# Fourteen of 48 row pairs of h kept in SBUF instead of six, and the projection written out with kept and loaded pairs in turn

## The chip, the cores and the metric

The kernel is one program on one core of a Trainium2 chip. The time is the device time of one execution in microseconds (us); three runs of the kernel before are the reference for it. Engines are called as in the profile: PE multiplies matrices (PEld is its loading of weights), DVE and ACT work on vectors, POOL is the fourth engine, and SP issues most of the DMA transfers. SBUF is the memory on the core, PSUM the one into which PE writes, HBM the memory outside.

## What is computed

The input x has 8 images, 48 channels, 96 rows and 96 columns. Two layers follow each other. The first runs a convolutional LSTM down the rows and a second one up the rows, projects the two states h of every row to 48 channels, normalises over the batch, applies relu and adds x:

```python
hs_f = _convlstm_scan(xr, w_f[:, :, 1, :], b_f, reverse=False)
hs_b = _convlstm_scan(xr, w_b[:, :, 1, :], b_b, reverse=True)
feats = jnp.concatenate([hs_f, hs_b], axis=2)
y = jnp.einsum('oc,bchw->bohw', w_proj, feats)
mu = jnp.mean(y, axis=(0, 2, 3)); var = jnp.var(y, axis=(0, 2, 3))
y = gamma * (y - mu) * rsqrt(var + EPS) + beta
x1 = relu(y) + x
```

The second layer is a masked bottleneck on x1: a 1x1 convolution from 48 to 288 hidden channels of which 144 are chosen for each image, a 3x3 depthwise convolution, a 1x1 convolution back to 48, a mask, and x1 added.

```python
h = relu(bn1(conv1x1(x1, w_pw1))) * mask_dilate * vector[:, :, None, None]
h = relu(bnd(dwconv3x3(h, w_dw))) * mask
```

## The kernel before

The kernel is five stages with a barrier between each two: recurrence, projection, residual, gather, bottleneck.

**Recurrence.** 96 steps, each one row of the forward scan (partitions 0 to 63) and one row of the backward scan (partitions 64 to 127). A step's h is stored by SP (`store_h`, line 221). Rows are stored by pairs, 48 of them; one pair is 2 rows x 8 images x 96 columns of 128 partitions, 768 KB. A pair is complete only when both scans have passed it, so the first pairs are finished last. Pairs 0 to 2 and 45 to 47 go into SBUF (`h_kept`, 6 places at the start of the tensor `shared`, line 228); pairs 3 to 44 go to HBM (`h_rows`, line 230).

**Projection** (lines 491 to 582). Per row PE runs two matmuls, one for each half of the images, into one of eight PSUM banks (line 555; in the trace each such fp32 matmul shows as two MATMUL records, so a pair of rows is 8 records). ACT copies the bank into y (line 567), and DVE takes statistics of the row (line 578). The six kept pairs come first; then the 42 loaded ones, through four buffers `h_in` that SP fills (line 536). A load waits until PE is done with the pair that was in its buffer (`row_summed`), a pair's first matmul waits for its load (`h_loaded`). Two turns of four pairs and one more are written out, the other turns run in a loop. y is one tensor, [128, 4, 96 rows, 96].

**Residual** reads all of y twice and x_parts from HBM into `shared`. **Gather** prepares weights. **Bottleneck** (from line 1066) works in 12 chunks of 8 rows. PE runs, in an order written out by hand in lines 1294 to 1328, `pw1` (line 1211, 64 partitions of y by 128 columns of weights, one matmul for each half of the partitions), `pw1_b` (line 1221, four matmuls of 128 partitions by 32 columns), the taps of the depthwise convolution (line 1247) and `pw2` (lines 1269 to 1288). `pw1` and `pw1_b` read y directly: a chunk's ten rows as two jobs r = 0 and r = 1 of five rows each, that is 480 columns (`span`, line 1118), starting one row before the chunk's first.

Of the kernel before, what the change touches and what calls it, by code (L numbers as in the profile page):

```python
# [40 lines left out]
P = 128  # L41
# [18 lines left out]
KEPT = 3  # L60
KEPT_PX = 2 * B * W
CONSTS = 3 * P + HG + 2 * UNITS * UC
# [18 lines left out]
SHARED = max(2 * KEPT * KEPT_PX, WCOLS + 5 * H1_PX + CPX)  # L81


def carved(shared, at, *shape):

    size = 1
    for n in shape:
        size *= n
    flat = shared[:, at:at + size]
    if len(shape) == 1:  # L90
        return flat
    if len(shape) == 2:
        return flat.rearrange("p (a b) -> p a b", a=shape[0])
    return flat.rearrange("p (n a b c) -> p n a b c", n=shape[0], a=shape[1], b=shape[2])

# [7 lines left out]
def recurrence(nc, x_steps, w_gates, w_kinds, h_rows, x_lanes, x_parts, x_copied, h_kept, w_proj, wp, wp_loaded):  # L103
# [13 lines left out]
    with ExitStack() as ctx:  # L117
# [80 lines left out]
        def _(sp):  # L198
# [22 lines left out]
            def store_h(i, e):  # L221
                for d in range(2):
# [4 lines left out]
                    if isinstance(two, int) and not KEPT <= two < H // 2 - KEPT:  # L227
                        to = h_kept[own, two if two < KEPT else two - H // 2 + 2 * KEPT, row]
                    else:
                        to = h_rows[two, own, row]  # L230
# [260 lines left out]
def projection(nc, h_rows, h_kept, wp, wp_loaded, y, stats):  # L491

    ROWS, BUFS = 2, 4
    TURN = ROWS * BUFS
    TURNS = H // TURN
    HERE = 2 * KEPT
    SHORT = -(-HERE // BUFS)
    with ExitStack() as ctx:
# [4 lines left out]
        ps = ctx.enter_context(nc.psum_tensor("proj", [P, TURN, 512], F32))  # L503
# [4 lines left out]
        def pair_at(i, n):  # L508

            if isinstance(i, int) and BUFS * i + n < HERE:  # L510
                place = BUFS * i + n
                return place if place < KEPT else place - HERE + H // 2
            return i * BUFS + (n - KEPT)

        def row_at(i, k):
            return pair_at(i, k // ROWS) * ROWS + k % ROWS

        def loads_before(i, n):

            return i - sum(1 for j in range(SHORT) if BUFS * j + n < HERE)  # L520

        def turns(eng, body):
            for i in range(SHORT + 1):
                body(i)
            with eng.Fori(SHORT + 1, TURNS) as i:
                body(i)

        @block.sync
        def _(sp):
            def body(i):  # L530
                for n in range(BUFS):
                    if isinstance(i, int) and BUFS * i + n < HERE:
                        continue
                    if not isinstance(i, int) or loads_before(i, n):
                        sp.wait_ge(row_summed, TURN * (i - 1) + ROWS * (n + 1))
                    sp.dma_start(h_in[n][:], h_rows[pair_at(i, n)]).then_inc(h_loaded[n], 16)

            turns(sp, body)

        @block.tensor  # L540
        def _(pe):
            pe.wait_ge(wp_loaded, 16)

            def body(i):
                for k in range(TURN):
                    n = k // ROWS
                    if isinstance(i, int) and BUFS * i + n < HERE:
                        h = h_kept[:, BUFS * i + n]
                    else:
                        h = h_in[n]  # L550
                        if k % ROWS == 0:
                            pe.wait_ge(h_loaded[n], 16 * (loads_before(i, n) + 1))
                    at_least(pe, row_kept, TURN * (i - 1) + k + 1)
                    for half in range(2):
                        mm = nc.tensor.matmul(ps[64 * half:64 * half + 64, k, 0:NH], wp[:],
                                              h[:, k % ROWS, HB * half:HB * half + HB, :],
                                              start=True, stop=True)
                    mm.then_inc(row_summed, 1)

            turns(pe, body)  # L560

        @block.scalar
        def _(act):
            def body(i):
                for k in range(TURN):
                    act.wait_ge(row_summed, TURN * i + k + 1)
                    nc.scalar.activation(y[:, :, bass.ds(row_at(i, k), 1), :],
                                         ps[:, k, 0:NH].rearrange("p (b r w) -> p b r w", b=HB, r=1),
                                         ACT.Identity).then_inc(row_kept, 1)

            turns(act, body)

        @block.vector
        def _(dve):
            def body(i):
                for k in range(TURN):
                    dve.wait_ge(row_kept, TURN * i + k + 1)
                    nc.vector.bn_stats(stats[:, bass.ds(row_at(i, k) * 6, 6)],
                                       y[:, :, bass.ds(row_at(i, k), 1), :]).then_inc(row_measured, 1)

            turns(dve, body)
            dve.wait_ge(row_measured, H)

def residual(nc, shared, y, stats, consts, norms, x_parts, x_copied, sums, folded, prefetch, w_mask, b_mask, mask_rows, masks_stored,
# [10 lines left out]
    with ExitStack() as ctx:  # L597
# [52 lines left out]
        def own(i):  # L650
            return y[:, i % HB].rearrange("p r w -> p (r w)")[:, i // HB * PART:(i // HB + 1) * PART]
# [142 lines left out]
        def _(pe):  # L794
# [5 lines left out]
            def block_of(j, pairs):  # L800
                for pair in pairs:
                    for half in range(2):
                        lanes = slice(64 * half, 64 * half + 64)
                        mm = nc.tensor.matmul(logits[32 * pair:32 * pair + 32, half, :], w_one[lanes, 31 - j:63 - j],
                                              y[lanes, pair].rearrange("p r w -> p (r w)")[:, BLOCK * j:BLOCK * (j + 1)],
# [260 lines left out]
def bottleneck(nc, shared, y, out_lanes, packs, passes, mask_rows, masks_stored):  # L1066
# [8 lines left out]
    with ExitStack() as ctx:  # L1075
# [93 lines left out]
        def _(sp):  # L1169
# [4 lines left out]
            def masks(o):  # L1174
                for n in range(ALL_Z):
# [7 lines left out]
                    if o == 0:  # L1183

                        if c:
# [3 lines left out]
                                     y[0:HI + C, GROUPS[g]].rearrange("p r w -> p (r w)")[:, at:at + CPX]  # L1189
# [12 lines left out]
        def _(pe):  # L1202
            def one_pass(o):
# [495 lines left out]
```

## Time and profile before

| | |
|---|---|
| Time, median of 3 runs | 1727.27 us (1725.79 to 1729.94) |
| Span of the profiled execution | 1727.3 us |
| PE busy | 1616.2 us (94%) |
| ACT busy | 1264.7 us (73%) |
| DVE busy | 1192.9 us (69%) |
| Issues of h_in<-h_rows | 42 of 768 KB, 6.3 us to landing (median) |
| Issues of h_rows<-h_new | 168 of 192 KB, 2.7 us to landing (median) |

The profiled execution's own time is its span, 1727.3 us, which is the median of the runs to within 0.1 us, so nothing has to be added to a sum made against it. By the timeline, the recurrence ends with the barrier before 993.9 us, the projection runs from there to the barrier before 1090.9 us, the residual and gather stages to about 1188.9 us, and the bottleneck to the end. In the tables of windows DMA share is the mean busy share of the 16 DMA engines (sampling can put it a little over 1), and PEclk is the clock that PE was granted, 1.00 being 2.4 GHz and 0.50 being 1.2 GHz. A MATMUL record's own duration contains its fill and drain; the spacing of starts tells how fast PE goes through them.

### The profile page before, as it was taken

What the parts mean: (1) busy time and instruction counts of PE and PEld (TensorE: products, weight loads), DVE (VectorE), ACT (ScalarE), POOL (GpSimd) and SP (SyncE); (2) the same over time, 40 slices, a digit from 0 to 9 for tenths busy, and PEclk for the clock granted to TensorE, in tenths of its full rate; (3) what the DMA queues carried; (4) which work ended last, traced back from release to release, by engine and by line L of the source; (5) the groups of instructions that cost most, each with busy time, mean ns of one, the idle gap of its engine ahead of it and who ended that gap; (6) DMA issues with size and microseconds to landing.
All of it is one profiled execution on the core that took longest, in us unless ns stands there. A gap on an engine that the chain in (4) does not pass through costs nothing. (4 is left out here: it accounts for less than half of the span.)

```text
span 1727.3 us, 57365 instructions
## 1 busy us (share of the span) xinstructions
PE 1616.2 (94%) x23474; PEld 1246.9 (72%) x23474; DVE 1192.9 (69%) x1989; ACT 1264.7 (73%) x2393; POOL 110.9 (6%) x189
## 2 busy tenths in 40 slices
PE   6999999999999999999999877467999999999996
PEld 6999999999999999999999832124444444444443
DVE  5777777777777777777777655775666666666664
ACT  5888888888888888888888844754665566565563
POOL 4000000000000000000000000000000000000000
PEclk9999999999999999999999989776999999999998
DMA  5666566566666666666666489840233333333334
GB/s 149 167 170 165 156 170 167 165 161 170 176 168 165 165 169 163 170 167 163 162 172 168 120 314 389 342 185 14 61 81 80 80 81 80 81 80 81 78 82 89
DMA packets 97151, 257.69 MB, mean 149 GB/s; under 512 B 23048, under 2 KB 29084, under 8 KB 96924
## 3 DMA queue, kind: packets, MB, share of 16 engines
q1 hardware_dynamic: 85496, 219.86, 43.7%
q0 software_dynamic: 10880, 35.40, 10.1%
q8 instruction: 106, 1.74, 0.4%
q10 hardware_dynamic: 644, 0.49, 0.1%
q14 instruction: 25, 0.20, 0.0%
HBM read 127.03 MB, written 85.08 MB: 123 GB/s over the span
## 5 line engine op out<-in xcount | busy, mean ns | idle before, releaser
L288 PE MATMUL gates<-state,w_high 64*128 64x384 f32 x4608 | 504.4, 337 | 0.0
L288 PEld LDWEIGHTS gates<-state,w_high 64*128 64x128 f32 x4608 | 416.5, 185 | 0.0
L1247 PE MATMUL psd<-shared 32*32 32x384 f32 x10368 | 296.8, 491 | 2.1 <-issue 1.0
L288 PE MATMUL gates<-state,w_low 64*128 64x384 f32 x2304 | 267.6, 337 | 0.0
L1247 PEld LDWEIGHTS psd<-shared 32*32 32x32 f32 x10368 | 161.9, 103 | 135.6 <-issue 81.6
L288 PE MATMUL gates<-x_both,w_high 64*128 64x384 f32 x2304 | 237.3, 338 | 13.7 <-ACT w_high L342 13.7
L347 ACT ACTIVATE sig_f<-gates 48x384 f32<-48x384 f32 x384 | 187.0, 487 | 48.0 <-PE gates L288 42.8
L288 PEld LDWEIGHTS gates<-x_both,w_high 64*128 64x128 f32 x2304 | 207.5, 186 | 13.7 <-ACT w_high L342 13.7
L288 PEld LDWEIGHTS gates<-state,w_low 64*128 64x128 f32 x2304 | 208.6, 185 | 0.0
L1485 DVE SCALAR_TENSOR_TENSOR acc<-shared,acc 128x768 f32<-128x768 f32 x144 | 146.5, 1018 | 81.7 <-ACT acc L1395 77.9
L1485 DVE SCALAR_TENSOR_TENSOR acc<-h,shared,acc 128x768 f32<-128x768 f32 x144 | 146.5, 1017 | 73.7 <-ACT acc L1395 69.8
L347 ACT ACTIVATE sig_o<-gates 48x384 f32<-48x384 f32 x384 | 187.2, 487 | 7.0
L443 DVE TENSOR_TENSOR h_new<-sig_o,tanh_c 128x384 f32<-128x384 f32 x192 | 107.2, 558 | 122.3 <-ACT tanh_c L365 122.3
L347 ACT ACTIVATE sig_i<-gates 48x384 f32<-48x384 f32 x384 | 185.9, 484 | 7.0
L347 ACT ACTIVATE tanh_g<-gates 48x384 f32<-48x384 f32 x384 | 185.7, 484 | 7.0
L1367 ACT ACTIVATE shared<-ps,shared 128x480 f32<-128x480 f32 (+1 forms) x176 | 123.4, 744 | 71.7 <-PE ps L1217 52.2
L432 DVE TENSOR_TENSOR i_g<-sig_i,tanh_g 128x384 f32<-128x384 f32 x192 | 107.2, 558 | 93.6 <-ACT tanh_g L347 93.6
L365 ACT ACTIVATE tanh_c<-cell 128x384 f32<-128x384 f32 x192 | 100.8, 525 | 53.1 <-DVE cell L435 53.1
L435 DVE TENSOR_TENSOR cell<-f_c,i_g 128x384 f32<-128x384 f32 x192 | 107.2, 558 | 20.0
L396 DVE TENSOR_TENSOR state<-h_new,state 128x384 fp32r<-128x384 f32 x192 | 107.2, 558 | 6.7
L428 DVE TENSOR_TENSOR f_c<-sig_f,cell 128x384 f32<-128x384 f32 x192 | 105.9, 551 | 5.4 <-ACT sig_f L347 5.4
L1217 PE MATMUL ps<-y,shared 64*128 64x480 f32 (+1 forms) x380 | 102.9, 612 | 5.4 <-SPq L1170 3.5
(153 smaller groups left out, 1620.8 us busy)
## 6 DMA issues: line engine op xcount, KB each, us to landing
x_taps<-x_both SPq DMA_DIRECT2D x192, 195.5 KB, 3.3
x_raw<-x_steps SPq DMA_DIRECT2D x192, 192.0 KB, 3.2
h_rows<-h_new SPq DMA_DIRECT2D x168, 192.0 KB, 2.7
h_in<-h_rows SPq DMA_DIRECT2D x42, 768.0 KB, 6.3
x_last<-x_both SPq DMA_DIRECT2D x192, 98.0 KB, 3.0
shared<-x_parts SPq DMA_DIRECT2D x24, 768.0 KB, 9.3
out<-y SPq DMA_DIRECT2D x48, 336.0 KB, 5.5
out<-z POOLq DMA_DIRECT2D x47, 336.0 KB, 5.6
```

Of the source, the lines that this page charges most:

```text
L288: return nc.tensor.matmul(gates[p][d][:, m, 0:NH], w[own, n, m, :], moving[own], start=start, stop=stop)
L347: return nc.scalar.activation(out[at], gates[p][d][col:col + HC, m, 0:NH].rearrange("p (b w) -> p b w", b=HB), func)
L365: nc.scalar.activation(tanh_c[p][:], cell[p][:], ACT.Tanh).then_inc(tc_ready, 1)
L396: nc.vector.tensor_tensor(state[1 - e][:, 1, b, 1:1 + W], h_new[e][:, b], state[1 - e][:, 0, b, 1:1 + W].bitcast(F32), ALU.subtract).then_ ...
L428: nc.vector.tensor_tensor(f_c[p][:], sig_f[p][:], cell[p][:], ALU.mult).then_inc(fc_ready, 1)
L432: nc.vector.tensor_tensor(i_g[p][:], sig_i[p][:], tanh_g[p][:], ALU.mult).then_inc(ig_ready, 1)
L435: nc.vector.tensor_tensor(cell[p][:], f_c[p][:], i_g[p][:], ALU.add).then_inc(cell_ready, 1)
L443: nc.vector.tensor_tensor(h_new[e][:, halves(p)], sig_o[e][:, halves(p)], tanh_c[p][:], ALU.mult).then_inc(h_ready, 1)
L1217: mm = nc.tensor.matmul(bank_of(j, half)[:, 0:(hi - lo) * W], wt[own, W_A + P * pair:W_A + P * (pair + 1)], y[own, pair, lo:hi, :], start= ...
L1247: mm = nc.tensor.matmul(psd[lane:lane + 32, 2 * x + i, 0:NH], wt[own, to:to + 32], h1p[2 * (s % 2) + x][own, dy + 4 * m:dy + 4 * m + 4, dx ...
L1367: return nc.scalar.activation(h1[:, first:first + hi - lo, 1:1 + W], bank[:, 0:(hi - lo) * W].rearrange("p (r w) -> p r w", w=W), ACT.Relu ...
L1485: nc.vector.scalar_tensor_tensor(a, window(h1d[d % 2], tap), par(D_UNITS[s], TAP + tap), a, ALU.mult, ALU.add).then_inc(acc_done if tap == ...
```

## The change

`KEPT` goes from 3 to 7, so pairs 0 to 6 and 41 to 47 stay in SBUF and 34 pairs are written to HBM and loaded. y becomes two tensors: `y_head` with rows 0 to 63 and `y_tail` with rows 64 to 95. y_tail is allocated before the recurrence, and the first eight kept places lie in it (`IN_TAIL` = 8); the other six lie in `shared`, whose size is unchanged. The projection is written out fully for PE, ACT, DVE and SP, in the order of a list: two kept pairs, then twelve times two loaded pairs and a kept one, then ten loaded pairs. Where the bottleneck reads rows on both sides of row 64, one matmul becomes two.

```diff
-KEPT = 3
+KEPT = 7
 KEPT_PX = 2 * B * W
+HEAD = 64
+IN_TAIL = (H - HEAD) * HB * W // KEPT_PX
...
-SHARED = max(2 * KEPT * KEPT_PX, WCOLS + 5 * H1_PX + CPX)
+SHARED = max((2 * KEPT - IN_TAIL) * KEPT_PX, WCOLS + 5 * H1_PX + CPX)
...
+def y_rows(y, lanes, pair, lo, hi):
+    head, tail = y
+    runs = []
+    if lo < HEAD:
+        runs.append((0, head[lanes, pair, lo:min(hi, HEAD), :]))
+    if hi > HEAD:
+        first = max(lo, HEAD)
+        runs.append(((first - lo) * W, tail[lanes, pair, first - HEAD:hi - HEAD, :]))
+    return [(at, ap, ap.shape[1] * W) for at, ap in runs]
...
+    ORDER = [("kept", 0), ("kept", 1)]
+    for n, pair in enumerate(LOADED):
+        ORDER.append(("loaded", pair))
+        if n % 2 == 1 and 2 + n // 2 < HERE:
+            ORDER.append(("kept", 2 + n // 2))
...
+            for pair in LOADED:
+                n = USE[pair]
+                if n >= BUFS:
+                    sp.wait_ge(row_summed, ROWS * (AT[pair - BUFS] + 1))
+                sp.dma_start(h_in[n % BUFS][:], h_rows[pair]).then_inc(h_loaded[n % BUFS], 16)
...
+            for k in range(H):
+                kind, n = ORDER[k // ROWS]
+                if kind == "kept":
+                    h = h_kept(n)
+                else:
+                    h = h_in[USE[n] % BUFS]
+                    if k % ROWS == 0:
+                        pe.wait_ge(h_loaded[USE[n] % BUFS], 16 * (USE[n] // BUFS + 1))
+                at_least(pe, row_kept, k - BANKS + 1)
+                for half in range(2):
+                    mm = nc.tensor.matmul(ps[64 * half:64 * half + 64, k % BANKS, 0:NH], wp[:],
+                                          h[:, k % ROWS, HB * half:HB * half + HB, :],
+                                          start=True, stop=True)
+                mm.then_inc(row_summed, 1)
...
-                        mm = nc.tensor.matmul(bank_of(j, half)[:, 0:(hi - lo) * W], wt[own, W_A + P * pair:W_A + P * (pair + 1)],
-                                              y[own, pair, lo:hi, :], start=True, stop=True)
+                        for at, x1, count in y_rows(y, own, pair, lo, hi):
+                            mm = nc.tensor.matmul(bank_of(j, half)[:, at:at + count], wt[own, W_A + P * pair:W_A + P * (pair + 1)],
+                                                  x1, start=True, stop=True)
...
+            if place < IN_TAIL:
+                flat = y_tail[:].rearrange("p b r w -> p (b r w)")[:, place * KEPT_PX:(place + 1) * KEPT_PX]
+            else:
+                flat = shared[:, (place - IN_TAIL) * KEPT_PX:(place - IN_TAIL + 1) * KEPT_PX]
```

`pw1_b` changes in the same way as `pw1`; the logits of the residual stage and the stores of y read blocks that row 64 never divides. Of the ten loaded pairs at the end, the first is pair 31.

PE at the start of the projection, before (`proj` are the PSUM banks, `shared` holds the kept pairs, `h_in` the loaded ones; a row of the list is one or more matmuls of the program):

```order
160 L555 MATMUL proj<-shared,wp 64x384 [waits wp_loaded]
161 L555 MATMUL proj<-shared,wp 64x384 x15
162 L555 MATMUL proj<-shared,wp 64x384 [waits row_kept]
163 L555 MATMUL proj<-shared,wp 64x384
164 L555 MATMUL proj<-shared,wp 64x384 [waits row_kept]
165 L555 MATMUL proj<-shared,wp 64x384
166 L555 MATMUL proj<-shared,wp 64x384 [waits row_kept]
167 L555 MATMUL proj<-shared,wp 64x384
168 L555 MATMUL proj<-shared,wp 64x384 [waits row_kept]
169 L555 MATMUL proj<-shared,wp 64x384
170 L555 MATMUL proj<-h_in,wp 64x384 [waits row_kept,h_loaded2]
171 L555 MATMUL proj<-h_in,wp 64x384
```

and now (`y_tail` holds kept pairs here):

```order
160 L579 MATMUL proj<-y_tail,wp 64x384 [waits wp_loaded]
161 L579 MATMUL proj<-y_tail,wp 64x384 x7
162 L579 MATMUL proj<-h_in,wp 64x384 [waits h_loaded0]
163 L579 MATMUL proj<-h_in,wp 64x384 x3
164 L579 MATMUL proj<-h_in,wp 64x384 [waits h_loaded1]
165 L579 MATMUL proj<-h_in,wp 64x384 x3
166 L579 MATMUL proj<-y_tail,wp 64x384 [waits row_kept]
167 L579 MATMUL proj<-y_tail,wp 64x384
168 L579 MATMUL proj<-y_tail,wp 64x384 [waits row_kept]
169 L579 MATMUL proj<-y_tail,wp 64x384
170 L579 MATMUL proj<-h_in,wp 64x384 [waits row_kept,h_loaded2]
171 L579 MATMUL proj<-h_in,wp 64x384
```

Six kept pairs, 24 matmuls, stood ahead of the first loaded pair; now two kept pairs, 8 matmuls, do, and from there each third pair is a kept one.

SP at the same place, before (`h_rows` is in HBM):

```order
149 L536 DMA h_in<-h_rows 128x1536 x4
150 L536 DMA h_in<-h_rows 128x1536 [waits row_summed] x2
151 L525 UNCONDITIONAL_BRANCH
152 L525 ISA
153 L536 ISA [waits row_summed]
154 L536 DMA h_in<-h_rows 128x1536
155 L535 REGISTER_ALU
156 L536 ISA [waits row_summed]
157 L536 DMA h_in<-h_rows 128x1536
158 L535 REGISTER_ALU
159 L536 ISA [waits row_summed]
```

and now:

```order
259 L148 UNCONDITIONAL_BRANCH [waits h_stored1,h_stored0]
260 L557 UNCONDITIONAL_BRANCH [waits barrier_Pool_Activation_PE_DVE_SP_release]
261 L564 DMA h_in<-h_rows 128x1536 x4
262 L564 DMA h_in<-h_rows 128x1536 [waits row_summed] x30
263 L538 UNCONDITIONAL_BRANCH
```

Four loads still go out without a wait, and the rest with a wait each. Of these there were 38; now there are 30.

PE in the bottleneck where job r = 1 of a chunk ends at row 64, before (`ps` and `psd` are PSUM, `shared` holds weights and the depthwise input):

```order
579 L1247 MATMUL psd<-shared 32x384 [waits relu2p_done,relu1_done]
580 L1247 MATMUL psd<-shared 32x384 x47
581 L1217 MATMUL ps<-y,shared 128x480 [waits relu1_done] x2
582 L1247 MATMUL psd<-shared 32x384 x96
583 L1217 MATMUL ps<-y,shared 128x480 [waits relu1_done] x2
```

and the same place now:

```order
757 L1262 MATMUL psd<-shared 32x384 x47
758 L1231 MATMUL ps<-y_head,shared 128x384 [waits relu1_done]
759 L1231 MATMUL ps<-y_tail,shared 128x96
760 L1231 MATMUL ps<-y_head,shared 128x384 [waits relu1_done]
761 L1231 MATMUL ps<-y_tail,shared 128x96
762 L1262 MATMUL psd<-shared 32x384 x96
763 L1231 MATMUL ps<-y_head,shared 128x96 [waits relu1_done]
764 L1231 MATMUL ps<-y_tail,shared 128x384
765 L1231 MATMUL ps<-y_head,shared 128x96 [waits relu1_done]
766 L1231 MATMUL ps<-y_tail,shared 128x384
```

The matmul of 480 columns of each half has become one of 384 and one of 96, with the same weights; both pieces of one half stand ahead of the first piece of the other half. The next job's are 96 and then 384.

## Rows read from the trace of the kernel before

**Rows 1.** Windows: stretch, its us, busy us, PEclk, DMA share, GB/s

```profile
core 0: us, PE busy (x) PEld busy (x) DVE busy (x) ACT busy (x) POOL busy (x), PEclk, DMA share, GB/s
1010.00:1015.00 5.00, 3.76 (x14) 1.51 (x16) 0.93 (x2) 1.02 (x3) 0.00 (x0) 0.66 0.92 385
...
1050.00:1060.00 10.00, 7.50 (x42) 2.50 (x40) 5.37 (x10) 4.90 (x10) 0.00 (x0) 1.00 1.00 400
...
1495.00:1538.00 43.00, 43.00 (x988) 19.53 (x984) 27.81 (x28) 25.95 (x39) 3.27 (x4) 1.00 0.39 81
```

**Rows 2.** Waits, 994 to 1091: total us, times, longest

```profile
PE proj L555 <- DMA h_in<-h_rows: 17.6, 28, 2.5
```

**Rows 3.** Timeline of PE, projection: start, us, instructions, idle before

```profile
993.95 9.59 PE L555 MATMUL proj<-shared,wp 128*64 128x384 f32 x48 [7.82 <-PEq L117]
1003.36 5.34 PE L555 MATMUL proj<-h_in,wp 128*64 128x384 f32 x32
1011.24 7.24 PE L555 MATMUL proj<-h_in,wp 128*64 128x384 f32 x32 [2.54 <-DMA h_in<-h_rows]
...
1029.48 1.51 PE L555 MATMUL proj<-h_in,wp 128*64 128x384 f32 x8 [1.60 <-DMA h_in<-h_rows]
1031.88 1.51 PE L555 MATMUL proj<-h_in,wp 128*64 128x384 f32 x8 [0.89 <-DMA h_in<-h_rows]
...
1087.47 1.51 PE L555 MATMUL proj<-h_in,wp 128*64 128x384 f32 x8 [0.45 <-DMA h_in<-h_rows]
```

**Rows 4.** Timeline, all engines, start of projection

```profile
995.53 0.49 ACT L567 ACTIVATE y<-proj 128x384 f32<-128x384 f32 x1 [6.17 <-PE proj L555]
...
998.42 0.49 ACT L567 ACTIVATE y<-proj 128x384 f32<-128x384 f32 x1 [0.15 <-PE proj L555]
...
1008.74 0.49 ACT L567 ACTIVATE y<-proj 128x384 f32<-128x384 f32 x1 [0.15 <-PE proj L555]
```

**Rows 5.** Timeline, SP's second batch of loads

```profile
1004.86 4.37 SPq L536 DMA_DIRECT2D h_in<-h_rows  x4
```

**Rows 6.** Landing of h_in loads issued 993.9, 995.2, and 1040 to 1060

```profile
DMA to landing us min/median/max: 4.4/4.4/4.4
...
DMA to landing us min/median/max: 7.3/8.0/8.7
...
DMA to landing us min/median/max: 5.8/6.1/6.5
```

**Rows 7.** Timeline of PE, bottleneck: two widths of line 1217, and 1226

```profile
1202.52 0.92 PE L1217 MATMUL ps<-y,shared 64*128 64x384 f32 x4
...
1206.07 1.07 PE L1217 MATMUL ps<-y,shared 64*128 64x480 f32 x4
...
1227.65 1.82 PE L1226 MATMUL ps<-y,shared 128*32 128x480 f32 x16
```

**Rows 8.** Chain of waits, 1560 to 1580: start, us, what

```profile
1567.53 1.00 PE ps L1217 x4
...
1572.92 1.75 PE ps L1226 x16
```

**Rows 9.** Waits of PE, 1200 to the end, longest of five

```profile
PE psd L1247 <- issue: 1.0, 3, 0.6
```

**Rows 10.** Timeline of PE, small matmuls of line 959

```profile
1183.95 1.51 PE L959 MATMUL ps_tail<-par,onehot_b 96*32 96x64 f32 x48
```

**Rows 11.** Timeline of PEld, weights for one pair of line 1217

```profile
1206.07 0.30 PEld L1217 LDWEIGHTS ps<-y,shared 64*128 64x128 f32 x4 [0.62 <-ACT shared L1367]
```

**Rows 12.** DMA issues 25 to 900: count, KB, us to landing

```profile
h_rows<-h_new SPq DMA_DIRECT2D x160, 192.0 KB, 2.7
...
shared<-h_new SPq DMA_DIRECT2D x12, 192.0 KB, 3.3
```

**Rows 13.** DMA queue of instructions, 1300 to 1400: packets, MB

```profile
q8 instruction: 18, 0.29, 1.2%
```

**Rows 14.** Windows, 1300 to 1400, columns as in rows 1

```profile
1300.00:1400.00 100.00, 99.78 (x2337) 45.80 (x2316) 68.58 (x70) 59.42 (x88) 8.18 (x10) 1.00 0.38 80
```

More of the change, by code:

```diff
@@ L94, in carved, with y_flat, kept_pair, kept_place @@
     return flat.rearrange("p (n a b c) -> p n a b c", n=shape[0], a=shape[1], b=shape[2])
+def y_rows(y, lanes, pair, lo, hi):
[7 more added lines that the diff above has]
+    return [(at, ap, ap.shape[1] * W) for at, ap in runs]
+def y_flat(y, lanes, pair, at, count):
+    head, tail = y
+    part, base = (head, 0) if at < HEAD * W else (tail, HEAD * W)
+    return part[lanes, pair].rearrange("p r w -> p (r w)")[:, at - base:at - base + count]
+def kept_pair(place):
+    return place if place < KEPT else place - 2 * KEPT + H // 2
+def kept_place(pair):
+    return pair if pair < KEPT else pair - H // 2 + 2 * KEPT
 def at_least(eng, sem, value):
@@ L227, in store_h @@
                     if isinstance(two, int) and not KEPT <= two < H // 2 - KEPT:
-                        to = h_kept[own, two if two < KEPT else two - H // 2 + 2 * KEPT, row]
+                        to = h_kept(kept_place(two))[own, row]
                     else:
@@ L491, in projection @@
 def projection(nc, h_rows, h_kept, wp, wp_loaded, y, stats):
-    ROWS, BUFS = 2, 4
-    TURN = ROWS * BUFS
-    TURNS = H // TURN
+    ROWS, BUFS, BANKS = 2, 4, 8
     HERE = 2 * KEPT
-    SHORT = -(-HERE // BUFS)
+    LOADED = range(KEPT, H // 2 - KEPT)
+    ORDER = [("kept", 0), ("kept", 1)]
[3 more added lines that the diff above has]
+            ORDER.append(("kept", 2 + n // 2))
+    assert sum(1 for kind, _ in ORDER if kind == "kept") == HERE and len(ORDER) == H // 2
+    USE = {pair: n for n, pair in enumerate(LOADED)}
+    AT = {pair: n for n, (kind, pair) in enumerate(ORDER) if kind == "loaded"}
     with ExitStack() as ctx:
@@ L506, in projection, with row_of, y_row @@
         block = ctx.enter_context(nc.Block())
[L508 to L526, printed above, removed]
+        def row_of(k):
+            kind, n = ORDER[k // ROWS]
+            return (n if kind == "loaded" else kept_pair(n)) * ROWS + k % ROWS
+        def y_row(row):
+            head, tail = y
+            return head[:, :, row, :] if row < HEAD else tail[:, :, row - HEAD, :]
         @block.sync
         def _(sp):
[L530 to L538, printed above, removed]
+            for pair in LOADED:
[3 more added lines that the diff above has]
+                sp.dma_start(h_in[n % BUFS][:], h_rows[pair]).then_inc(h_loaded[n % BUFS], 16)
         @block.tensor
@@ L542, in _ @@
             pe.wait_ge(wp_loaded, 16)
[L544 to L558, printed above, removed]
@@ L562, in _ @@
         @block.scalar
         def _(act):
[L564 to L571, printed above, removed]
+            for k in range(H):
+                act.wait_ge(row_summed, k + 1)
+                nc.scalar.activation(y_row(row_of(k)), ps[:, k % BANKS, 0:NH].rearrange("p (b w) -> p b w", b=HB),
+                                     ACT.Identity).then_inc(row_kept, 1)
@@ L573, in _ @@
         @block.vector
         def _(dve):
[L575 to L581, printed above, removed]
+            for k in range(H):
+                dve.wait_ge(row_kept, k + 1)
+                nc.vector.bn_stats(stats[:, 6 * row_of(k):6 * row_of(k) + 6], y_row(row_of(k))).then_inc(row_measured, 1)
@@ L1225, in pw1_b @@
                         for pair in range(HB):
[L1226 to L1228 removed]
+                            for at, x1, count in y_rows(y, slice(0, P), pair, lo, hi):
+                                mm = nc.tensor.matmul(bank_of(job_b(c), r)[32 * pair:32 * pair + 32, at:at + count],
+                                                      wt[:, W_B + 32 * pair:W_B + 32 * (pair + 1)],
+                                                      x1, start=True, stop=True)
                     mm.then_inc(pw1_done, 1)
```

20 lines of the change are left out of this document (10 added, 10 removed).

## The prediction

> **What bounds the kernel now.** I read the slices of the page first, then a table of windows, then waits and timeline of the two places that the change touches. In the windows the reader is to see two different kernels. In the projection, from 1050 to 1060, the DMA engines are busy all of the time at 400 GB/s and PE only 7.50 us of 10; in the bottleneck, from 1495 to 1538, PE is busy 43.00 of 43 us and the DMA share is 0.39 [rows 1]. So in the projection bytes count, in the bottleneck PE's instructions. The waits agree: in the projection PE waits 17.6 us in 28 pieces for h_in [rows 2], while from 1200 on the longest total of its waits is 1.0 us [rows 9].
>
> The timeline of PE gives the rhythm of the projection [rows 3]. Six kept pairs and the first four loaded ones run from 993.95 to 1008.7 without a wait. Then come two bursts of four pairs, starting at 1011.24 and, after 18.24 us for eight pairs, at 1029.48: 2.28 us a pair. From 1031.88 to the last pair at 1087.47 the 29 pairs start one by one, 28 steps of 1.985 us, each held by its load. That is the steady rate of the loads. The bursts are a result of the order: the first four loads all went out at once, the second four only at 1004.86 and after, since PE was busy with kept pairs [rows 5]; the last of the first four landed by 995.2 + 8.7 = 1003.9 [rows 6], so for a while no load was under way, and later four buffers ran in step. In a burst the clock is low as well: 0.66 from 1010 to 1015, a mix of 1.2 and 2.4 GHz [rows 1].
>
> PE's own rate: ACT copies each row as PE finishes it, at 998.42 and again at 1008.74, 16 rows later, so 0.645 us a row or 1.29 us a pair at 2.4 GHz [rows 4]. The first copy stands at 995.53, 1.6 us after PE's start, at the low clock.
>
> **The projection, step by step.** Removed are 8 of 42 loads. What ends the stage is then the later of two chains.
> - The loads. The first one lands at 993.9 + 4.4 = 998.3 [rows 6]; two kept pairs cover it, since their four rows are done about then [rows 4]. With 1.985 us for each of the other 33 the last pair can start at 998.3 + 33 x 1.985 = 1063.8. Before it started at 1087.47 [rows 3]. Gain 23.7 us.
> - PE. From row 4 on there are 92 rows of 0.645 us = 59.3 us after 998.4; its last pair would start at 998.4 + 59.3 - 1.3 = 1056.4, which is 31.1 us earlier than before. It is the end of the range on the fast side, if the loads ran so fast.
>
> Why the loads should stay at their steady rate: the interleaving asks of them two pairs in the time in which PE does three, 3.87 us, and they need 2 x 1.985 = 3.97 us. So both are busy nearly all of the time. From PE's release of a buffer until PE wants it again lie three loaded pairs and two kept ones, 5 x 1.29 = 6.45 us, and a load of the steady phase lands after 5.8 to 6.5 us [rows 6]. It fits with nothing to spare, so I let the loads decide. In the ten loaded pairs at the end nothing lies between; that is the steady phase of before. The bad end is the rate of the bursts throughout: 998.3 + 33 x 2.28 = 1073.5, gain 14.0 us. I take 1.985, for it comes from 28 steps under the same queue.
>
> The Trainium skill, in DMA: Bandwidth & Descriptors (the table at its head), gives about 358 GB/s as one core's limit from HBM. The trace disagrees: 400 GB/s over 10 us [rows 1], and the measurement decides. By the page's figure a pair of 786,432 bytes would take 2.20 us, an estimate, the last pair would start at 1070.9, and the gain would be 16.6 us.
>
> The tail behind the last pair (copy, statistics, barrier) is the same code and moves with it. Writing the loop out takes register instructions off ACT and DVE, which wait for PE anyway: nothing.
>
> **Stores in the recurrence.** Eight more pairs, 32 stores of 192 KB, go to SBUF. Such a store lands after 3.3 us against 2.7 us to HBM [rows 12], and is next waited for a pair of steps later, some 20 us. Same count, same queue, same place: nothing, with 1 us to either side. The last store before the barrier went to SBUF before too.
>
> **The bottleneck: what the split of y costs.** Rows 60 to 64 (chunk 7, r = 1) and 63 to 67 (chunk 8, r = 0) lie across row 64. That makes 2 x 4 pairs of `pw1`, two halves each, and 2 x 4 matmuls of `pw1_b`: 24 matmuls become 48. PE has no waits there to hide them, so each us is lost. No row shows two matmuls of one part of the array in a row ahead of the other part's, so I bound.
> - Widths: a `pw1` job of 384 columns has 0.92 us in the timeline, one of 480 columns 1.07 us [rows 7], so 96 columns are about 0.16 us; the job takes 1.00 us of the chain [rows 8], that is 0.80 of columns with both halves side by side and 0.20 fixed.
> - If the second half can't start until the first half's second piece does: 384 then 96 takes 0.64 + 0.64 + 0.16 + 0.20 = 1.64 instead of 1.00, so 0.64 more; 96 then 384 takes 0.16 + 0.16 + 0.64 + 0.20 = 1.16, 0.16 more. Four of each: 3.2 us. `pw1_b` takes 1.75 us for both r [rows 8], four matmuls side by side in 0.80 of columns. In turn, they become 4 x 0.64 + 0.16 = 2.72 (1.92 more) and 4 x 0.16 + 0.64 = 1.28 (0.48 more): 2.4 us. Together 5.6 us.
> - Low end: the pieces run as freely as the 24 small matmuls of line 959, 1.51 us for 24 [rows 10]: 1.5 us. High end: the serial 5.6 us, and the weights of the 16 added `pw1` pieces, 0.30 us for two halves [rows 11], uncovered: 8 x 0.30 = 2.4, so 8.0 us.
>
> I take 5.6 us: PE is given its matmuls in program order, and the two pieces of one half need the same part of the array.
>
> On this the Trainium skill has two rules that point in two directions. TensorE: Matmul & The Clock Gate (Part 3, what overlaps) says that matmuls start and end in program order and that a weight load passes running matmuls only in another row group; by that the sum holds 5.6 us or more. TensorEngine Tiling (Key Properties) says that tiles work independently of each other; by that it would hold nearer 1.5 us. No run so far shows which.
>
> **Sum.** 1727.3 (span, equal to the median) - 23.7 + 5.6 = 1709.2 us.
>
> **Rivals.**
> - *Fast.* The pieces overlap (1.5 us) and the loads hold 1.985: 1727.3 - 23.7 + 1.5 = 1705.1. With PE as the bound of the projection instead, 1727.3 - 31.1 + 1.5 = 1697.7. For it speaks that the four records of a `pw1` job load all their weights within 0.30 us [rows 11]; against the second part, that the DMA engines were full already at 400 GB/s.
> - *Bursts stay.* If uneven release of buffers (two pairs 1.29 us apart, then a gap) keeps the loads at 2.28 us: 1727.3 - 14.0 + 5.6 = 1718.9. For it: 18 us of this in the trace. Against: it followed a gap with no load under way, and the new order has none.
> - *Slower: instruction blocks.* The written-out projection streams its instructions by DMA, behind the loads. In the bottleneck 18 packets came for 2337 + 2316 + 70 + 88 instructions [rows 13, 14], about 270 each; the projection has 768 of PE and 192 of ACT and DVE and so brings 4 packets or more. If each was late by a load's landing, 6.3 us, and they added up, that is 25 us and the time 1709.2 + 25 = 1734. It decides from three late packets on (18.1 us of net gain / 6.3). Against: the first 24 rows are written out already, and their PE rows run at 0.645 us without a gap [rows 4].
> - *No change to speak of.* A gain at the low end with a late packet or two: 1718.9 + 6.3 = 1725.
>
> **Chances.** Forecast 1709 as it stands: 0.52. Fast: 0.25. Bursts stay: 0.15. No change: 0.04. Slower: 0.04. Runs of this kernel lie within 0.2%, about 3.5 us, of each other, and within that is no change. Faster 0.92, same 0.04, slower 0.04. For 8 in 10 the range takes the forecast with the ends of the split (1705 to 1712), goes down into the fast case without all of PE's bound, and up to the bursts: 1701 to 1719.
>
> **What will show it.** The kernel is right step by step if the last loaded pair starts near 1063.8 and loads go at 1.9 to 2.0 us each; if no PE gap lies between 998 and the first turns, with PEclk 1.00 from there; if `pw1` with two pieces takes 1.6 us in chunk 7 and 1.2 in chunk 8, `pw1_b` 2.7 and 1.3; and if chunks 0 to 6 and 9 to 11 and the recurrence keep their lengths. The prediction is wrong if a load takes 2.2 us or more, if ACT or PE stand still in the projection with no semaphore to wait for, or if the recurrence is longer.

## The result and the profile after

The changed kernel takes 1709.1 us (median of 4 runs, 1708.4 to 1711.0) against 1726.6 us of the kernel before (median of 4); the ratio is 0.9894 with a 95% interval of 0.988 to 0.9908. Two later comparisons (e9_again and e10_after_3, below) gave 0.9902 (0.9873 to 0.9931) and 0.991 (0.9883 to 0.9936), so the medians differ by 14 to 17 us. The profiled execution has a span of 1706.6 us and took 1708.7 us.

PE's timeline in the projection, kernel after (start, us, what, idle time before and what ended it), answers to [rows 3]:

```profile
991.66 5.32 PE L579 MATMUL proj<-y_tail,wp 128*64 128x384 f32 x16 [7.83 <-PEq L148]
996.79 2.76 PE L579 MATMUL proj<-h_in,wp 128*64 128x384 f32 x16
999.38 1.47 PE L579 MATMUL proj<-y_tail,wp 128*64 128x384 f32 x8
...
1044.96 1.46 PE L579 MATMUL proj<-shared,wp 128*64 128x384 f32 x8
1046.25 2.75 PE L579 MATMUL proj<-h_in,wp 128*64 128x384 f32 x16
1050.04 1.51 PE L579 MATMUL proj<-h_in,wp 128*64 128x384 f32 x8 [1.04 <-DMA h_in<-h_rows]
1051.91 1.51 PE L579 MATMUL proj<-h_in,wp 128*64 128x384 f32 x8 [0.35 <-DMA h_in<-h_rows]
...
1063.68 1.51 PE L579 MATMUL proj<-h_in,wp 128*64 128x384 f32 x8 [0.37 <-DMA h_in<-h_rows]
```

The first load is there when two kept pairs are done, nothing waits at 996.79, and the last pair starts 72.0 us after PE's first matmul, where it was 93.5. The waits of PE between 991 and 1065, against [rows 2]:

```profile
PE proj L579 <- DMA h_in<-h_rows: 5.6, 12, 1.0
```

The 17.6 us in 28 pieces are 5.6 in 12. Windows of the interleaved part (columns as in [rows 1]):

```profile
1011.66:1031.66 20.00, 19.39 (x120) 8.07 (x118) 16.74 (x31) 14.70 (x30) 0.00 (x0) 1.00 0.96 372
1031.66:1051.66 20.00, 18.55 (x112) 7.40 (x108) 15.25 (x28) 13.29 (x28) 0.00 (x0) 1.00 0.98 386
```

PE is busy 93 to 97% there, where it was 75% [rows 1], and the DMA engines still are busy almost all of the time. In the bottleneck, the two jobs that lie across row 64, in the timeline of PE after:

```profile
1494.84 0.92 PE L1231 MATMUL ps<-y_head,shared 64*128 64x384 f32 x4
1495.59 0.37 PE L1231 MATMUL ps<-y_tail,shared 64*128 64x96 f32 x4
1495.89 5.30 PE L1262 MATMUL psd<-shared 32*32 32x384 f32 x192
1501.12 0.47 PE L1231 MATMUL ps<-y_head,shared 64*128 64x96 f32 x4
1501.41 0.85 PE L1231 MATMUL ps<-y_tail,shared 64*128 64x384 f32 x4
...
1509.88 0.39 PE L1241 MATMUL ps<-y_head,shared 128*32 128x96 f32 x8
1510.07 1.65 PE L1241 MATMUL ps<-y_tail,shared 128*32 128x384 f32 x16
1511.65 1.15 PE L1262 MATMUL psd<-shared 32*32 32x384 f32 x33
```

From a job's first record to the next instruction it takes 1.05 us (384 then 96 columns) and 1.07 us (1501.12 to 1502.19, 96 then 384), `pw1_b` 1.77 us; undivided they took 1.00 and 1.75 [rows 8]. The forecast was 1.64 and 1.16 for the two orders of pieces, and 1.75 + 0.48 = 2.23 for this `pw1_b`, of whose two jobs one is divided, 96 columns first.

By stages, the first pair of profiles, in us:

| | before | after | difference |
|---|---|---|---|
| Recurrence, up to PE's first projection matmul | 993.95 | 991.66 | -2.3 |
| Projection, from there to bn_aggr | 97.0 | 75.2 | -21.8 |
| Residual and gather, to the first pw1 | 98.0 | 98.1 | +0.1 |
| Bottleneck, to the end | 538.3 | 541.6 | +3.3 |

One execution is too little for this. Over all profiles of this study PE's first projection matmul came between 990.4 and 994.1 with either store pattern (991.6 and 994.1 in two kernels with the old recurrence, 993.4 and 992.9 in two more executions of the changed one), so the -2.3 is the execution's. For the projection three profiles with the old code (97.0, 95.1, 94.5) stand against three with the new (75.2, 76.3, 76.4): 95.5 against 76.0, a gain of 19.6 us. (A fourth profile with the old order and the old 42 loads, e5_unroll_only below, had 97.9; with it the gain is 20.2.)

### The profile page after: what moved, and what is told of

Same layout as the page of the kernel before. It is cut to its first block and busy times, and to the rows that moved or that the text cites. A ratio compares the mean times of both kernels' runs of the same rounds, so it can differ in the third digit from the quotient of the medians.

```text
span 1706.6 us, 56613 instructions
## 1 busy us (share of the span) xinstructions
PE 1613.0 (95%) x23522; PEld 1253.0 (73%) x23522; DVE 1193.5 (70%) x1989; ACT 1265.0 (74%) x2393; POOL 110.5 (6%) x189
## 5 line engine op out<-in xcount | busy, mean ns | idle before, releaser
L1500 DVE SCALAR_TENSOR_TENSOR acc<-h,shared,acc 128x768 f32<-128x768 f32 x144 | 146.5, 1018 | 73.3 <-ACT acc L1410 69.4
L1382 ACT ACTIVATE shared<-ps,shared 128x480 f32<-128x480 f32 (+1 forms) x176 | 123.3, 743 | 72.3 <-PE ps L1231 52.8
L319 PE MATMUL gates<-x_last,w_low 64*128 64x384 f32 x768 | 102.1, 344 | 1.0 <-DMA x_last<-x_both 0.6
```

What stands on the lines that cost most here:

```text
L319: return nc.tensor.matmul(gates[p][d][:, m, 0:NH], w[own, n, m, :], moving[own], start=start, stop=stop)
L1382: return nc.scalar.activation(h1[:, first:first + hi - lo, 1:1 + W], bank[:, 0:(hi - lo) * W].rearrange("p (r w) -> p r w", w=W), ACT.Relu ...
L1500: nc.vector.scalar_tensor_tensor(a, window(h1d[d % 2], tap), par(D_UNITS[s], TAP + tap), a, ALU.mult, ALU.add).then_inc(acc_done if tap == ...
```

## The experiments

Each was compared with the kernel before on its own chip. "Last pair" is the start of the last loaded pair after PE's first matmul of the projection, "projection" the time from that matmul to bn_aggr, "bottleneck" the time from the first `pw1` to the end; these three are of one profiled execution each. The kernel before took 1728.2 us beside e1, e2, e4 and e5, 1728.1 us beside e3, e6, e8 and e9, and 1727.4 us beside e10 and v1.

| | time, us | ratio to before, 95% | last pair | projection | bottleneck |
|---|---|---|---|---|---|
| e1_split_all | 1738.1 | 1.0054 (1.0039 to 1.0069) | 91.7 | 95.1 | 552.5 |
| e2_split_64 | 1730.9 | 1.0016 (1.0003 to 1.0029) | 91.0 | 94.5 | 540.9 |
| e5_unroll_only | 1729.0 | 1.0009 (0.9994 to 1.0023) | 94.7 | 97.9 | 540.1 |
| e4_order_only | 1724.1 | 0.9988 (0.9969 to 1.0008) | 86.5 | 89.6 | 543.9 |
| e3_kept_first | 1725.2 | 0.9979 (0.9962 to 0.9996) | 86.0 | 89.2 | 540.3 |
| e6_half_bytes | 1701.0 | 0.9835 (0.9806 to 0.9864) | 62.6 | 66.1 | 542.0 |
| e8_bufs3 | 1727.1 | 0.999 (0.9975 to 1.0005) | 87.9 | 91.0 | 544.4 |
| e9_again (the changed kernel) | 1712.3 | 0.9902 (0.9873 to 0.9931) | 73.2 | 76.3 | 543.4 |
| e10_after_3 (the changed kernel) | 1713.2 | 0.991 (0.9883 to 0.9936) | 73.3 | 76.4 | 543.9 |
| v1_keep18 | 1705.5 | 0.9864 (0.9838 to 0.989) | 66.3 | 69.5 | 545.4 |

### What the split of y costs

e1_split_all, on the kernel before:

```diff
-mm = nc.tensor.matmul(bank_of(j, half)[:, 0:(hi - lo) * W], wt[own, ...], y[own, pair, lo:hi, :], ...)
+mid = lo + 1 if r == 0 else hi - 1
+for a, b in [(lo, mid), (mid, hi)]:
+    mm = nc.tensor.matmul(bank_of(j, half)[:, (a - lo) * W:(b - lo) * W], wt[own, ...], y[own, pair, a:b, :], ...)
```

and the same in `pw1_b`. In e2_split_64 only the jobs across row 64 are cut, there.

> The kernel before, with nothing changed but this: in every chunk of the bottleneck each matmul of pw1 and of pw1_b is cut into two pieces, 96 columns and the rest (r = 0) or the rest and 96 (r = 1). All 12 chunks then pay what the changed kernel pays for two jobs' rows. Theory A (pieces of one part of the array hold up the other parts, as the prediction had it): about 0.16 us more per pw1 job at r = 0, 0.64 at r = 1 and 2.4 for both jobs of pw1_b, so 12 x (4 x 0.16 + 4 x 0.64 + 2.4) = about 67 us more than before, 1794 us. Theory B (each part of the array works through its own pieces, from the changed kernel's trace about 0.05 us per pw1 job and next to nothing for pw1_b): 96 x 0.05 = about 5 us more, 1732 us. In between, at some 0.2 us per job, it would be 20 us.

> The kernel before, with only the matmuls that lie across row 64 of y cut there (chunk 7 r = 1, chunk 8 r = 0), so the changed kernel's 24 added matmuls and nothing else of it. Theory A (serial pieces): 5.6 us more than before, 1733 us. Theory B (independent parts): 0.5 us more, not to be told from 0. The changed kernel's bottleneck was 3.3 us longer in its profile; if the split is the cause of that in some other way than by its own duration, it shows here as 3 us.

Cutting all twelve chunks costs 9.3 us (6.7 to 11.9), not 67: 0.78 us (0.56 to 0.99) for a chunk's 24 added matmuls, and 24 added matmuls are all that the change has. The timeline of PE in e1_split_all:

```profile
1401.71 1.87 PE L1233 MATMUL ps<-y,shared 128*32 128x96 f32 x32
1403.51 4.33 PE L1254 MATMUL psd<-shared 32*32 32x384 f32 x128
1407.77 1.15 PE L1222 MATMUL ps<-y,shared 64*128 64x96 f32 x8
1408.85 0.54 PE L1276 MATMUL ps<-h2p,shared 64*64 64x384 f32 x2
```

`pw1_b` takes 1.80 us to the next instruction, a `pw1` job 1.08: some 0.05 and 0.08 more than undivided [rows 8], and 8 x 0.08 + 0.05 = 0.7 a chunk. The serial theory is refuted. e2_split_64 came out 2.8 us slower (0.5 to 5.0), which excludes 5.6, and from 0.78 can't be told.

### Order, number of loads and the written-out code

```diff
 e5_unroll_only, on the kernel after
-KEPT = 7
+KEPT = 3
-IN_TAIL = (H - HEAD) * HB * W // KEPT_PX
+IN_TAIL = 0
-ORDER = [two kept, then two loaded and a kept one in turn]
+ORDER = [("kept", n) for n in range(HERE)] + [("loaded", pair) for pair in LOADED]
```

e4_order_only has the first two edits alone, e3_kept_first the last alone.

> The changed kernel with 6 kept pairs as before, none in y's tail, and the kept ones projected first: the order and the bytes of before, written out instead of looped, and y still split. Theory A (written-out code costs nothing, as its instructions come ahead of need): within 1 us of before, last pair 93.5 us after PE's first matmul of the projection. Theory B (instruction blocks come late behind the loads): one to four waits of some 6 us, 1733 us or more. Theory C (the loop itself cost something per pair, so part of the gain came from its end): faster than before by 1 to 4 us.

> The changed kernel with 6 kept pairs as before (42 loads, none in y's tail), but in the new interleaved order: two kept, then loaded ones with a kept one after every second until the kept ones are used up. Theory A (the loads run without a break from the first landing on, 1.985 us each): the last pair starts at 998.3 + 41 x 1.985 = 1079.7 on the scale of before, 7.8 us earlier than before, so about 1720 us. Theory B (only the number of loads counts and the order is worth nothing): as before, 1727. If the four-pair bursts at 2.28 us stay, 998.3 + 41 x 2.28 = 1091.8, so 1732.

> The changed kernel with all 14 kept pairs projected first and the 34 loaded ones after them; same bytes, same stores, same code otherwise. Theory A (the gain needs the interleaving, since the loads stand still once four buffers are full): PE starts the first loaded pair after 28 rows of 0.645 us = some 19 us, 4 loads are there, and 30 more have to follow at 1.985 us from then on, so the last pair starts some 13 us later than in the changed kernel, 1722 us; with bursts at 2.28 us for the first eight some 15 us. Theory B (eight loads fewer are worth 8 x 1.985 = 16 us whatever the order): 1711 us, and no more than 2 us over the changed kernel.

Written out, the old order takes the old time (between 1.0 us less and 4.0 more), so the loop cost nothing and no instruction block came late; "Slower" is refuted. The new order with the old 42 loads starts the last pair 8.2 us earlier than e5, as expected (7.8), though its time is only 4.9 us less; against the kernel before the time alone doesn't show a gain (ratio 0.9969 to 1.0008). Eight fewer loads in the old order bring 2.9 us (0.7 to 6.6 by the interval of the ratio) instead of 14 to 17; with all kept pairs first the kernel is 12.8 us slower than e9_again on the same chip, where theory A had 13. The timeline of PE in e3_kept_first shows why:

```profile
993.29 12.56 PE L575 MATMUL proj<-y_tail,wp 128*64 128x384 f32 x64 [7.83 <-PEq L148]
1005.68 7.92 PE L575 MATMUL proj<-shared,wp 128*64 128x384 f32 x48
1013.42 5.34 PE L575 MATMUL proj<-h_in,wp 128*64 128x384 f32 x32
```

and its windows of the same stretch (columns as in [rows 1]):

```profile
1003.29:1008.29 5.00, 5.00 (x34) 2.33 (x32) 4.38 (x8) 3.89 (x8) 0.00 (x0) 1.00 0.01 2
1008.29:1013.29 5.00, 5.00 (x34) 2.42 (x32) 4.35 (x8) 3.76 (x9) 0.00 (x0) 1.00 0.00 0
```

For ten microseconds nothing is loaded: all four buffers are full and PE is busy with kept pairs. The kept pairs are worth their loads where they lie between the loaded ones. With the old order most of what they save goes into a longer gap.

### What bounds the new projection

```diff
 e6_half_bytes, on the kernel after (leaves out half of the loaded bytes)
-sp.dma_start(h_in[n % BUFS][:], h_rows[pair])
+sp.dma_start(h_in[n % BUFS][:, 0:1], h_rows[pair, :, 0:1])
-h[:, k % ROWS, ...]
+h[:, 0 if kind == "loaded" else k % ROWS, ...]
 e8_bufs3, on the kernel after
-ROWS, BUFS, BANKS = 2, 4, 8
+ROWS, BUFS, BANKS = 2, 3, 8
```

> The changed kernel, but each load brings only the first row of its pair, and the second row's matmuls read the first row again: half of the loaded bytes and half of the loaded rows are left out, the matmuls and their order are the same. Theory A (the loads bound the projection): PE becomes the bound, 0.645 us a row, and the last pair starts at 1056.4 on the scale of before, 7.3 us earlier than in the changed kernel, so about 1702 us. Theory B (PE was the bound of most of it already and the loads cost only its last ten pairs): those ten go from 1.89 to 1.29 us each, 6 us, 1703 us; the two differ in where the time goes: by A before and in the last ten pairs, by B in the last ten alone. Theory C (latency or the rhythm of buffers bounds it, not bytes): less than 2 us gained.

> The changed kernel with three buffers for loaded pairs instead of four. Theory A (three loads under way are enough to keep the DMA engines full, bytes decide): within 2 us of the changed kernel. Theory B (a load's own time of 6.4 us from issue to landing decides: with three buffers a load can start only after the third pair before it was projected, so a pair of loads' time is (6.4 + 1.29) / 3 = 2.56 us where nothing lies between): the last ten pairs go from 1.89 to about 2.5 us, 6 us, and the interleaved part loses too; 10 to 20 us in all, 1719 to 1729 us.

With half of the bytes PE doesn't wait for a load at all, and the time is 11.3 us less than that of e9_again on the same chip, so theory C is refuted. PE's timeline ends:

```profile
1042.16 1.47 PE L579 MATMUL proj<-shared,wp 128*64 128x384 f32 x8
1043.45 13.42 PE L579 MATMUL proj<-h_in,wp 128*64 128x384 f32 x80
```

Ten pairs at 1.29 us, the last at 1043.45 + 9 x 1.29 = 1055.1, 62.6 us after PE's first matmul; the forecast floor was 1056.4 - 993.95 = 62.5. The changed kernel is 10 us above it: it reaches the ten last pairs after 54.6 us (1046.25) where e6 needs 51.0, and spends 17.4 us on nine steps where e6 spends 11.6. So theory A holds: the loads bound both parts, the last ten pairs more. What e6 doesn't separate is bytes and waiting time, since its loads also landed sooner, after 3.7 us instead of 6.4.

Three buffers cost 14.8 us against e9_again on the same chip. In the last pairs (timeline of PE in e8_bufs3)

```profile
1061.84 1.51 PE L579 MATMUL proj<-h_in,wp 128*64 128x384 f32 x8 [0.56 <-DMA h_in<-h_rows]
...
1079.38 1.51 PE L579 MATMUL proj<-h_in,wp 128*64 128x384 f32 x8 [0.42 <-DMA h_in<-h_rows]
```

seven steps take 17.54 us, 2.51 each (expected 2.56); singly they are 1.9 to 3.2 us. The DMA engines are not full there (windows):

```profile
1061.84:1079.38 17.54, 10.58 (x57) 3.40 (x57) 7.79 (x14) 6.75 (x14) 0.00 (x0) 1.00 0.82 306
```

and a load still takes 5.9 us to land (median of the 34), not much less than the 6.4 with four buffers. So with three buffers the time from issue to landing decides, as theory B had it; A is refuted. That with four it is the bytes rests on the DMA share of 0.96 to 0.98 in the changed kernel's windows; five buffers, which would have settled it, were not tried.

### Run to run

> The changed kernel again, for a second profile of it. The recurrence was 2.3 us shorter in its profile than in that of the kernel before, the bottleneck 3.3 us longer; if these are the run's own, they vary here by about that (recurrence up to PE's first projection matmul at 991.7 to 994), and the clock rows at the bottleneck's start with them. If they belong to the change they stand: 991.7 and 541.6 us.

> The changed kernel on the same chip as the version with 18 kept pairs, so that the two can be compared directly: 1709 to 1712 us, last pair 72 to 73.2 us after PE's start.

The recurrence varied as expected and the projection stood. The time of e10_after_3, 1713.2 us, lies a little above the expected 1709 to 1712. The bottleneck did not come back to 541.6: 543.4 and 543.9. Its parts show two places. In the first chunk, the windows of 20 us that begin 20 us after its first matmul, kernel after:

```profile
1184.97:1204.97 20.00, 19.12 (x441) 9.50 (x456) 15.88 (x16) 14.84 (x24) 0.88 (x1) 0.91 0.08 13
```

and e9_again:

```profile
1187.64:1207.64 20.00, 19.69 (x499) 9.66 (x498) 17.14 (x17) 13.52 (x22) 0.88 (x1) 1.00 0.18 36
```

A mean granted clock of 0.91, a mix of the two levels of 1.2 and 2.4 GHz, instead of 1.00 goes with a first chunk of 38.3 us instead of 35.6; the first profile of the changed kernel and e10_after_3 had it, the others not. And the last stretch, from the twelfth `pw1_b` to the end, took 67.0 and 66.9 us in the first two profiles and 67.7 to 72.3 in the others. The traces show what is longer there: DVE's idle time, most of it for transfers. The last three outputs in the timeline of DVE, kernel before:

```profile
1706.20 1.02 DVE L1495 SCALAR_TENSOR_TENSOR z<-ps,shared,mask 128x768 f32<-128x768 f32 x1 [1.17 <-DMA mask<-mask_rows]
1710.54 1.02 DVE L1495 SCALAR_TENSOR_TENSOR acc<-ps,shared,mask 128x768 f32<-128x768 f32 x1 [3.32 <-PE ps L1286]
1715.79 1.02 DVE L1495 SCALAR_TENSOR_TENSOR z<-ps,shared,mask 128x768 f32<-128x768 f32 x1 [4.23 <-DMA mask<-mask_rows]
```

and e9_again:

```profile
1686.59 1.02 DVE L1510 SCALAR_TENSOR_TENSOR z<-ps,shared,mask 128x768 f32<-128x768 f32 x1 [3.36 <-DMA out<-z]
1692.96 1.02 DVE L1510 SCALAR_TENSOR_TENSOR acc<-ps,shared,mask 128x768 f32<-128x768 f32 x1 [5.34 <-DMA mask<-mask_rows]
1698.19 1.02 DVE L1510 SCALAR_TENSOR_TENSOR z<-ps,shared,mask 128x768 f32<-128x768 f32 x1 [4.21 <-DMA mask<-mask_rows]
```

That is 8.7 us of idle time against 12.9, and from the last of these outputs to the end it is 11.5 us against 12.8. The changed kernel's first profile, the same program as e9_again, had 9.9 and 11.2, so this is scatter from one execution to the next and not the change. Why the transfers land later in some executions is open. The four stretches from the eighth `pw1_b` to the twelfth, in which nearly all of the split lies, took 173.9 us before and 173.9, 174.0 and 174.1 in the three profiles of the changed kernel: what is late around row 64 (up to 1.3 us) is made up in the next chunks. Of the executions with kept pairs first, four had bottlenecks of 538.3 to 540.9; the seven with pairs in turn had 541.6 to 545.4. The fifth with kept pairs first is e1_split_all: its 552.5 less the 8 to 9 us of its cut matmuls is 543 to 544, in the other group. So the order is a doubtful cause; I know of no mechanism for it and tested none.

### A further version

```diff
 v1_keep18, on the kernel after
-KEPT = 7
-HEAD = 64
+KEPT = 9
+HEAD = 48
+PLACES = [45, 0, 1, 46, 2, 3, 47, 4, 5, 6, 7, 8, 39, 40, 41, 42, 43, 44]
...
+    kept = [p for p in range(IN_TAIL) if PLACES[p] < KEPT] + [p for p in range(IN_TAIL) if PLACES[p] > KEPT]
+    kept += range(IN_TAIL, HERE)
+    ORDER = [("kept", kept.pop(0)), ("kept", kept.pop(0))]
+    for n, pair in enumerate(LOADED):
+        ORDER.append(("loaded", pair))
+        if kept and (n < 2 * KEPT and n % 3 != 2 or n >= 2 * KEPT and n % 2 == 1):
+            ORDER.append(("kept", kept.pop(0)))
```

> A further version: 18 kept pairs instead of 14, 30 loaded; y is cut at row 48 instead of 64, its rows 48 to 95 hold 12 of the kept pairs until they are projected, and the order takes a kept pair after every loaded one or two at first (all 12 are read before y's row 48 or higher is written over them), so that loads and PE have about the same work. Theory (bytes bound the changed kernel's projection, PE's own floor is 9 to 10 us below, as with half of the bytes): the loads need 4.4 + 29 x 1.985 = 62.0 us from PE's start to the last pair's start, PE's own rows 62.6 us; with both this close some 64 us, against 72.0 and 73.2 of the changed kernel, so 8 to 9 us less, 1701 to 1704 us. The stores of 8 more rows' pairs to SBUF cost nothing and the cut of y 0.5 us as before. Rival (no rate but the number of kept pairs in the interleaving counts, or writing next to y's kept pairs adds waits): 4 loads less are worth 4 x 1.985 = 8 us only if PE keeps up, else nothing: 1710.

It takes 1705.5 us (five runs, 1698.7 to 1707.9) where the changed kernel takes 1713.2 (four, 1707.8 to 1714.1) on the same chip: 7.7 us less, where 8 to 9 less and 1701 to 1704 us had been expected. The last pair starts after 66.3 us, 2.3 us later than expected. Waits of PE, 990 to 1060:

```profile
PE proj L584 <- DMA h_in<-h_rows: 2.1, 5, 0.7
```

Little is left to gain from loads: PE's own floor of 62.6 us is 3.7 us away.

## Why the prediction was right, and where it was wrong

**Time: 1709.2 forecast, 1709.1 measured.** The mechanism of the gain was right: loads and kept pairs in turn, the loads as the bound. That of the cost of the split was wrong. The two terms were off by 4 to 5 us each in opposite directions, and the agreement to 0.1 us is chance.

**The basis.** I took the span of 1727.3 us as the execution's own time. In every execution for which both are known the time is 1.9 to 2.2 us above the span (1708.67 and 1706.6 here), so the profiled execution of before took about 1729.3 us, and is not the run of the median; the nearest of the reference runs is the one of 1729.94. The sum should have had 2 us added for that, and 2 us taken off again to reach the median; the two cancel.

**The loads, -23.7.** The step said 4.35 us to the first landing and 33 x 1.985 = 65.5, so 69.9 us to the last pair. Measured are 72.0, 73.2 and 73.3. The first landing is right (no wait at 996.79). The rate is not quite (nor was it the 2.20 us worked out from the Trainium skill, DMA: Bandwidth & Descriptors, the table at its head): (72.8 - 4.4) / 33 = 2.07 us a load over three profiles. That is 3.0 us, and it is the term that was mis-sized. The 1.985 was one execution's rate. From the 13th loaded pair to the last, 29 steps with nothing between, the kernels with the old order and 42 loads took 58.0 us (before), 57.5 (e1), 56.6 (e2) and 60.6 (e5), so 1.95 to 2.09 us a load; e4_order_only, with four kept pairs among its first loads, needs (1078.30 - 996.19) / 41 = 2.00. In the changed kernel the last seven steps, also with nothing between, took 1.95, 2.13 and 1.96 us each in the three profiles. So 2.07 lies within the scatter of the loads themselves, and whether the uneven release of buffers between kept pairs adds to it is not shown, though "it fits with nothing to spare" left no room for either. A further 1.5 us was in the kernel before: its profiled execution had 93.5 us to the last pair, two others 91.0 and 91.7. 23.7 - 3.0 - 1.5 = 19.2, and the profiles' means give 92.1 - 72.8 = 19.3.

**The bursts.** I read them as the result of the gap in the loads, and the low clock as something beside it. For the time that holds, for the pattern it doesn't. The eight pairs that took 18.24 us in two bursts, from the fifth loaded pair to the 13th, took 17.87 us in e1, 18.05 in e2 and 18.43 in e5, all three with the same order, singly and at a granted clock of 1.00. So 2.28 us a pair is the price of getting going again after the gap, and the bursts add nothing to it. What makes four pairs run together is the clock: in e3_kept_first a burst stands in the middle of a steady stretch, with no gap in the loads, behind a wait of 1.94 us of PE (timeline, then windows):

```profile
1044.80 7.18 PE L575 MATMUL proj<-h_in,wp 128*64 128x384 f32 x32 [1.94 <-DMA h_in<-h_rows]
```

```profile
1042.80:1044.80 2.00, 0.07 (x2) 0.00 (x0) 1.11 (x2) 0.49 (x1) 0.00 (x0) 1.00 1.02 418
1044.80:1048.80 4.00, 4.00 (x14) 1.57 (x16) 1.12 (x2) 1.18 (x3) 0.00 (x0) 0.57 0.91 350
1048.80:1052.80 4.00, 3.61 (x24) 1.31 (x22) 3.05 (x6) 2.74 (x6) 0.00 (x0) 1.00 0.98 330
```

PE came back at a granted clock of 0.57, between its levels of 1.2 and 2.4 GHz, after nearly standing still, and took four pairs without a wait; the next one started at 1052.37, after 7.57 us, which is four steps of 1.89. The burst cost nothing; the long step ahead of it did. A burst doesn't always follow: in e2_split_64 a wait of 2.25 us was followed by a granted clock of 1.00, and so was one of 1.92 us in the changed kernel (timeline, then windows of e10_after_3):

```profile
1052.47 1.51 PE L579 MATMUL proj<-h_in,wp 128*64 128x384 f32 x8 [1.92 <-DMA h_in<-h_rows]
```

```profile
1052.47:1056.47 4.00, 3.27 (x18) 1.16 (x20) 1.73 (x4) 1.96 (x4) 0.00 (x0) 1.00 1.01 349
```

"Bursts stay" at 2.28 us a load did not happen: the new order has no gap in the loads.

**The split, +5.6.** This term failed, at the step "PE is given its matmuls in program order, and the two pieces of one half need the same part of the array". Each half goes on by itself. In program order the first half's short piece stands ahead of the second half's long one. In the trace of the first job above the long pieces of both halves start together, one line of 0.92 us as in a job of 384 columns [rows 7], and the short ones of both start behind them, at 1495.59. The whole job takes 1.05 us, not 1.64. The price is 0.5 us by the changed kernel's own rows (8 jobs of 0.05 to 0.07 and 0.02 for `pw1_b`) and 0.8 us by e1_split_all; the "low end" of 1.5 was still too high. Of the two rules of the Trainium skill quoted in the prediction, TensorEngine Tiling (Key Properties), by which tiles work independently, agrees with these runs; the in-order rule of TensorE: Matmul & The Clock Gate (Part 3) is not what they show: the second half's long piece started about 0.7 us before the first half's short one. I should have given the independent case more than the 0.25 of "Fast", all the more as `pw1_b` was seen to run four matmuls side by side.

**Recurrence, code, residual.** All priced at nothing; the runs show nothing beyond their scatter. The fetching of instructions, which carried the slower rival, brought 3 packets in the new projection against 1 and no wait (e5_unroll_only).

**The balance.** -19.3 and +0.8 make -18.5 us; the three comparisons gave -17.4, -15.8 and -14.2. The profiles put the remaining 1 to 4 us into the bottleneck's first chunk (2.6 us in two of three, with the lower clock) and its end (4.6 us in one of three, with DVE's longer waits for transfers); whether they belong to the change or to the execution is open.

## What to carry to other kernels

Keeping data on the core saves transfer time only if the work on it lies between the transfers: eight pairs fewer to load brought about 3 us in one block ahead, 14 to 17 us in turn. Take the order from the two rates, so that neither side runs out, and count buffers against the time from issue to landing. Before pricing small matmuls in series, look whether neighbours on other parts of the array already run beside each other, and cut one up everywhere to measure it. And a stage's length from one profile has a scatter of its own: here up to 3 us of 95.

## What the runs showed of the hardware

- Halving the bytes of each load did not halve the DMA engines' work. In e6_half_bytes (windows):

```profile
1012.47:1032.47 20.00, 20.00 (x126) 9.64 (x124) 17.36 (x32) 15.23 (x32) 0.00 (x0) 1.00 0.73 204
```

  0.73 of the engines' time moved 204 GB/s, so 279 GB/s for a full share, against 372 / 0.96 = 388 GB/s in the changed kernel's window above. A load of 384 KB (3,072 bytes in a row per partition instead of 6,144) landed after 3.7 us, one of 768 KB after 6.4.
- Loads in a steady stretch come in steps of 1.89 us (786,432 bytes, so 416 GB/s), with longer ones of 2.0 to 3.4 us scattered among them, in e4_order_only after up to eleven short ones, in the kernel before also two in a row; the means of 1.95 to 2.13 are made of these.
- A matmul cut in two on one part of the array does not hold up the other part: a job of two halves, each cut in two, takes 0.05 to 0.08 us more (1.05 to 1.08 against 1.00).
